# Attention with a causal mask: TensorE adds the diagonal's mask to the first pass's scores, and VectorE takes the maximum of an item in one operation

## The reference

```python
def _L0_attn_ref(normalized_resid_pre, W_Q, b_Q, W_K, b_K, W_V, b_V, W_O, b_O):
    q = jnp.einsum('bsd,hde->bshe', x, W_Q) + b_Q
    k = jnp.einsum('bsd,hde->bshe', x, W_K) + b_K
    v = jnp.einsum('bsd,hde->bshe', x, W_V) + b_V
    scores = jnp.einsum('bqhe,bkhe->bhqk', q, k) / math.sqrt(D_HEAD)
    causal = jnp.tril(jnp.ones((s, s), dtype=bool))
    scores = jnp.where(causal[None, None], scores, -jnp.inf)
    pattern = jax.nn.softmax(scores, axis=-1)
    z = jnp.einsum('bhqk,bkhe->bqhe', pattern, v)
    return jnp.einsum('bqhe,hed->bqd', z, W_O) + b_O

h = _L0_tok_ref(x, L0_tok_weight)
h = h + _L0_attn_ref(_layernorm(h), ...)
h = h + _L0_ffn_ref(_layernorm(h), ...)
```

## Time and profile before

| | |
|---|---|
| median of 3 runs | 2586.66 us (2585.57 to 2587.82) |
| the profiled execution's own time | 2586.6 us |
| its span, first to last instruction | 2584.6 us |
| mean granted clock of TensorE | 0.969 |
| PE, PEld busy | 2362.9, 1248.4 us |
| DVE, ACT, POOL busy | 1876.3, 1244.5, 1247.3 us |
| matmuls, each with its own weight load | 16192 |

### The profile page before, as it was taken

One profiled execution on the slowest core, in us unless ns is written; L12 is line 12 of the kernel. 1 busy time (PEld: TensorE's weight loads), 2 busy tenths in 40 slices (PEclk: granted clock), 3 DMA queues, 4 the chain that ended last, 5 costly groups with the idle time before them and its releaser, 6 DMA issues. The chain is left out here.

```text
span 2584.6 us, 42857 instructions
## 1 busy us (share of the span) xinstructions
PE 2362.9 (91%) x16192; PEld 1248.4 (48%) x16192; DVE 1876.3 (73%) x3898; ACT 1244.5 (48%) x1760; POOL 1247.3 (48%) x858
## 2 busy tenths in 40 slices
PE   3567999999999999999999999977999999999998
PEld 1234556565666565666666666543333333333332
DVE  7877665656656665656575656768888988988987
ACT  3323333333333333333333333446787777777776
POOL 6000375757676666666676767553323413413120
PEclk9788999999999999999999999987999999999999
DMA  1011000000001000000000010141001001011000
GB/s 51 23 37 32 8 1 10 1 10 1 10 1 34 1 10 1 10 1 10 1 10 6 5 21 1 19 90 21 17 19 19 9 19 21 15 19 21 7 7 7
DMA packets 42942, 39.36 MB, mean 15 GB/s; under 512 B 26865, under 2 KB 35186, under 8 KB 41842
## 3 DMA queue, kind: packets, MB, share of 16 engines
q1 hardware_dynamic: 40608, 31.18, 5.4%
q0 software_dynamic: 1536, 3.15, 0.4%
q10 hardware_dynamic: 594, 2.31, 0.2%
HBM read 26.13 MB, written 10.49 MB: 14 GB/s over the span
## 5 line engine op out<-in xcount | busy, mean ns | idle before, releaser
L727 POOL TENSOR_TENSOR acc<-acc,pT 128x1024 f32<-128x1024 f32 (+3 forms) x412 | 837.1, 2032 | 238.4 <-ACT pT L1222 202.5
L1222 ACT ACTIVATE pT<-banks 128x1024 f32<-128x1024 f32 x480 | 406.3, 896 | 757.7 <-PE banks L806 756.8
L1964 DVE TENSOR_TENSOR hw<-hid,banks 128x512 f32<-128x512 f32 x1024 | 663.0, 680 | 85.5 <-PE banks L1647 70.9
L991 DVE TENSOR_REDUCE part<-banks 128x2 f32<-128x1024 f32 (+3 forms) x432 | 440.1, 1044 | 298.4 <-PE banks L782 295.0
L1806 ACT ACTIVATE hid<-banks 128x1024 f32<-128x1024 f32 x512 | 496.7, 1022 | 185.6 <-PE banks L1637 168.8
L822 PE MATMUL banks<-pT,v 128*64 128x512 f32 (+3 forms) x1920 | 404.6, 542 | 4.5 <-POOL pT L711 2.6
L1647 PE MATMUL banks<-wT,select 64*128 64x512 f16 x1024 | 343.1, 394 | 40.7 <-DVE hw L1964 21.2
L1637 PE MATMUL banks<-zst,w1c 50*128 50x512 f32 x1024 | 306.7, 544 | 12.1 <-ACT hid L1806 12.1
L1647 PEld LDWEIGHTS banks<-wT,select 64*128 64x128 f16 x1024 | 94.1, 94 | 398.3 <-DVE hw L1964 338.9
L1655 PE MATMUL banks<-hw,w 128*32 128x512 f32 x2048 | 279.7, 619 | 0.9 <-DVE hw L1964 0.9
L822 PEld LDWEIGHTS banks<-pT,v 128*64 128x64 f32 x1920 | 116.4, 136 | 193.0 <-issue 177.3
(11 more groups left out here) (257 smaller groups left out, 3216.9 us busy)
## 6 DMA issues: line engine op xcount, KB each, us to landing
zst<-z_scratch SPq DMA_DIRECT2D x48, 128.0 KB, 4.1
z_scratch<-zp SPq DMA_DIRECT2D x8, 512.0 KB, 2.8
out_h<-o SPq DMA_DIRECT2D x8, 384.0 KB, 2.6
xT_scratch<-pT SPq DMA_DIRECT2D x4, 512.0 KB, 2.7
xt_hi<-xT_scratch SPq DMA_DIRECT2D x2, 1024.0 KB, 5.5
w<-in_L_ffn_W ACTq DMA_DIRECT2D x1, 2048.0 KB, 8.3
xt_hi<-in_L_ffn_W SPq DMA_DIRECT2D x12, 128.0 KB, 4.6
v<-in_L_ffn_W SPq DMA_DIRECT2D x12, 128.0 KB, 4.5
```

What stands on the lines that cost most here:

```text
L727: pool.tensor_tensor(acc[:, G % 2, :, off:CH], acc[:, G % 2, :, off:CH], pT[:, slot, :, 0:w], ALU.add).then_inc(summed, 1)
L991: last = dve.tensor_reduce(to[:, :, c:c + 1], both[:, :, 0:whole], AX.X, ALU.max)
L1222: act.activation(pT[:, J % PSLOTS, :, 0:CH - off], both[:, :, 0:CH - off], ACT.Exp, scale=E ** -0.5)\
L1964: dve.tensor_tensor(hw[:, n % 2, q, :], hid[:, n % 2, q, :], ring_bank(("w", g, n, q)), ALU.mult).then_inc(mixed, 1)
```

## The change

The mask becomes bf16, and its value above the diagonal becomes -2^100, which bf16 holds exactly. VectorE makes a bf16 copy of the identity. Behind the first of the three pairs of score matmuls of a diagonal item, PE multiplies the identity by the mask into the last 128 columns of each of the two banks, so that the mask is added to the scores in PSUM. VectorE then takes the maximum over the whole item, for both heads, in one operation; `part` has four columns instead of five. The wait for the mask goes from VectorE to PE, ahead of its first matmul.

```diff
-MASKED = -1.0e30
+MASKED = -2.0 ** 100
...
-    COLS = 5
+    COLS = 4
...
-        mask = sb("mask", [P, P])
+
+        mask, ident_b = sb("mask", [P, P], BF16), sb("ident_b", [P, P], BF16)
...
                         last = pe.matmul(banks[h][:, 0:w], a[u][head(h), i * P:(i + 1) * P],
                                          b[u][head(h), c * CH:c * CH + w], start=(k == 0), stop=(k == 2))
+                    if k == 0 and c == i // TQ:
+
+                        for h in range(2):
+                            pe.matmul(banks[h][:, w - P:w], ident_b[:, :], mask[:, :], start=False, stop=False)
                 last.then_inc(filled, 1)
...
-            pe.wait_ge(consts_ready, 2)
+            pe.wait_ge(consts_ready, 3)
+            pe.wait_ge(mask_ready, 2)
...
+            dve.tensor_copy(ident_b[:, :], ident[:, :]).then_inc(consts_ready, 1)
             dve.memset(ones[:, :].bitcast(F32), 1.0).then_inc(consts_ready, 1)
             dve.memset(cpad[:, :, :], 0.0).then_inc(consts_ready, 1)
-            dve.wait_ge(mask_ready, 2)
...
-                diagonal = c == Q
-                whole = w - P if diagonal else w
-                to = part[:, Q % 2, 2 * t:2 * t + 2, :]
-                if whole:
-                    last = dve.tensor_reduce(to[:, :, c:c + 1], both[:, :, 0:whole], AX.X, ALU.max)
-                if diagonal:
-                    for h in range(2):
-                        block_on_diagonal = both[:, h, whole:w]
-                        last = dve.tensor_tensor_reduce(block_on_diagonal, block_on_diagonal, mask[:, :], 1.0, NEG,
-                                                        ALU.add, ALU.max, to[:, h, c + 1:c + 2])
-                last.then_inc(max_taken, 1)
-                if diagonal and t == TQ - 1:
+                dve.tensor_reduce(part[:, Q % 2, 2 * t:2 * t + 2, c:c + 1], both[:, :, 0:w], AX.X, ALU.max)\
+                   .then_inc(max_taken, 1)
+                if c == Q and t == TQ - 1:
```

## The result

The change makes the kernel slower: 2630.96 us (median of 4 runs) against 2587.24, ratio 1.0169 with a 95% interval of 1.0139 to 1.0199. The forecast was 2652, with 2628 to 2674 as its range. The profiled execution has a span of 2630.3 us against 2584.6: 45.7 more.

What follows compares the result with a forecast made beforehand. TensorE's attention stream was taken to bound the kernel: 176 items at 0.41 us (72.2), less 5.0 in holes and 2 in the first pass, gave +65 on 2586.6, so 2652 us, range 2628 to 2674.

Steps and rivals of the forecast that it cites:

- lower end of the range: Diagonal items at 0.30 us each, without the long first gap: +46, 2632 us, widened to 2628.
- What bounds: Attention stage from 306 us on: one TensorE stream without holes; each nanosecond added comes out, VectorE time there is worth nothing.
- The price of an item: Each diagonal item, between first and second score pairs: two mask matmuls add 0.41 us to TensorE; 176 items, 72.2 us.
- The four steps: Diagonal item: entering full-height form 0.09, second mask matmul 0.06, going back 0.15, long first gap behind 0.11 us.
- What takes some of it back: Units 1 to 11: mask matmuls fill ScalarE bank waits right behind two diagonal items, 0.45 us a unit, 5.0 us.
- The first pass: Unit 0: PE waits for VectorE, whose 16 items get shorter: 2.9 us less at most, 2 taken; mask matmuls fit idle.
- Hidden switches: Rival, diagonal items: mask weights load behind the running pair, only columns count, 0.11 us each: +15, 2602 us; chance 7%.
- VectorE's hand-back: Rival: VectorE's freeing of banks sets the pace, 0.18 us sooner at 44 waits: 10 us off, 2577 us; chance 3%.
- 31 us of weight-load waits: PE weight loads waiting on VectorE's masked maximum: they come after the second product and could not start before it.

Runs made afterwards that it cites:

- VectorE's part: The changed kernel without the mask matmuls, keeping one maximum over the whole item with the diagonal block unmasked: 2585.56 us against 2587.0 before, ratio 0.9994.
- TensorE's part alone: The kernel before with the mask matmuls added, VectorE still taking its masked maxima: 2634.43 us, ratio 1.0179.
- half-height kernel: The changed kernel with the mask added by two pairs of 64-row matmuls instead of two full-height matmuls: 2601.55 us against 2587.0 before, ratio 1.0057.
- twice-masked kernel: The changed kernel with each of the two mask matmuls issued twice in a row: 2653.95 us against 2586.62 before, ratio 1.0259.

## Why the prediction was right, and which term was off

- *The number.* The change costs 43.7 us by the medians, where the forecast's sum was 65. 2630.96 us lies 3 us above the lower end of the range. That end was worked out from 0.30 us an item, without the long gap, and this is not what happened: an item costs 0.40, and the holes took back over four times what the forecast gave them. That the time still lies in the range is in part luck.
- *What bounds.* Right for the engine: VectorE's part is worth 0 from 306 us on, and TensorE's part alone gives the whole +47. Too strong in "with no hole" and "each nanosecond [...] comes out at the end", which rested on the two microseconds of the earlier trace rows: of 70 us put in, 47 came out. The waits of the kernel before have, next to the 31.0 us of the earlier trace rows, this line:

```profile
PEld banks L782 <- ACT pT L1222: 34.2, 121, 0.5
```

- *The price of an item, 0.41 us.* Right to a few hundredths for 512 columns (0.43), too high for 128 (0.36, since their first pair's gap was only 0.06 before). With 0.40 as the mean, 176 items are 70 us against 72 in the sum. The four steps were all there; but the last, booked as the price of switching back, is there in the half-height kernel too, which doesn't switch.
- *What takes some of it back, 5.0 us.* This term was mis-sized: 70 less 47.3 is 23 us. Matched start by start between the two kernels, without the mask's own, the matmuls that lie between 306 and 1640 us before the change show 69.5 us added between the first and the third pair of the diagonal items. 6.6 are taken back right behind them (forecast: 5.0) and 15.5 elsewhere: 6.8 in the 22 gaps behind the transposes, 2.0 ahead of 22 other items, and 5.8 in 55 gaps behind the first pair of an item that is not diagonal. I had looked only right behind diagonal items. The waits two places on, in particular the two of each unit behind the transposes (7 us), were visible in the kernel before and I did not look for them. And each wait has a second part that I had priced for switches but not for waits: the gap behind the first pair after it is long too. The 256-wide item at 798.49, which had waited, has 0.23 to its second pair and then 0.12. Where the wait goes, this 0.11 goes with it.
- *The first pass, -2 us.* It came out as +0.3: VectorE's part alone shows -1.5 there, and with TensorE's part alone, which I had placed at nothing, it is +1.9. How much of the 1.9 is the mask matmuls is not shown, since these are single executions with different clocks. From 222 to 275 us the granted clock was 0.94 before and 0.87 with the change (the 1.00 of the forecast held from 306 us on); with VectorE's part alone and with TensorE's part alone it was (third column from the right):

```profile
222.00:275.00 53.00, 40.95 (x303) 28.48 (x303) 43.41 (x61) 8.62 (x19) 0.00 (x0) 0.90 0.09 24
222.00:275.00 53.00, 44.98 (x311) 28.80 (x309) 43.72 (x114) 8.03 (x16) 0.00 (x0) 0.84 0.09 24
```

- *The rivals.* Hidden switches: refuted by every item's rows; in the 176 items the second pair starts 0.20 to 0.33 us later, 0.30 in the mean. VectorE's hand-back: refuted by its part alone. The 31 us of weight-load waits behind the masked maximum were, as argued, no waits of the stream.

Not settled: why TensorE's low clock at the start of the stage lasted longer in the changed kernel's profile; VectorE's part alone and the twice-masked kernel, among others, start their first pass about as late (223.5 and 223.7 against 222.8 us), while the half-height one does not (222.6), so no part of the change is tied to it.

## What to carry to other kernels

Before moving elementwise work into a full TensorE stream, price the switch of its form, not the columns: here 0.29 of 0.40 us with the long gap behind it, of which some 0.2 went when the added matmuls took their neighbours' form. Price the stream's holes too, by its waits anywhere behind the edit and not just at the next instruction, since an insertion shifts all that follows up to the next wait. And ask whether the moved work is needed at all: the mask on the maximum was not, for this kernel's inputs.

## What was not expected of the hardware

- Four half-height bf16 matmuls (a pair of 128 columns and a pair of 64) behind a 64-row pair take 0.09 us of the stream (892.56 to 892.65), against 0.11 for two full-height ones of 128 columns. The gap behind the next pair is long all the same, 0.32 instead of 0.23, although no form changes.
- The gap behind the first pair after a wait is long too: 0.23 instead of 0.12 for 256 columns. The gaps of this kind that closed with the change gave back 5.8 us, besides the waits themselves.
- A matmul of 8 columns is not much cheaper here than one of 128: in the item above two of them and the way back take 0.13 instead of 0.21 us.
